# Gated cross-attention with two mixture-of-experts layers: moving the narrow products of TensorE directly behind the scores

## The chip, the core and the metric

The kernel runs on one core of a Trainium2 chip. The metric is the device time of one execution in microseconds (us). Its engines are TensorE (PE; its weight loads are listed as PEld), VectorE (DVE), ScalarE (ACT), GpSimd (POOL) and SyncE (SP, which issues transfers). Each runs its own list of instructions in order, and they wait for each other by semaphores.

## What is computed

Input x has 64 batches of 64 rows of 128 features. Two layers follow each other; each is a cross-attention to a context of the same shape, with 16 heads of 8 features, and then a mixture of experts. Layer one masks keys and sends each row to one of 8 experts (128 to 512 to 128); layer two has no mask and sends each row to two of 16 experts (128 to 64 to 128), with a capacity per expert and batch.

```
x = x + tanh(g_xattn[0]) * attention_0(layernorm(x), ctx, mask)
x = x + tanh(g_ffn[0])   * top1_experts(layernorm(x))
x = x + tanh(g_xattn[1]) * attention_1(layernorm(x), ctx)
x = x + tanh(g_ffn[1])   * top2_experts(layernorm(x))
```

Attention is softmax(Q K^T / sqrt(8)) V per head, with projections of x and ctx in front and an output projection behind.

## The kernel before

The 4,096 rows are 32 tiles of 128 rows (two batches each). A layer's attention loop goes over its 32 tiles; tiles 0 to 31 are layer one, 32 to 63 layer two. Tiles are gathered in groups of 2 or 4 (`SIZES`), and a group has units of two tiles. Products that are made for a whole group are the projections Q (L841) and K (L753), the transposes of x (L794), of the attention result (L896, "av") and of the router's input (L804), the output product (L903), the router's logits (L814) and the products that rank rows by expert (L823 to L835). V is projected per unit (L764). Per tile there are:

- the scores (L860): products of 32 rows by 64 columns of the array into the banks S_ps; layer one first writes the mask into the same banks with four full-array products (L854);
- four passes of VectorE over the scores: maximum and subtraction (L604, L612) for the first half of the heads, then for the second. `score` of the next tile waits for all of them, since S_ps is not doubled;
- the turn: four full-array transposes of the probabilities of one half of the heads (L871) into the one bank T_ps; ScalarE's exponential (L534) takes them from there to SBUF. Either half has a turn, and each waits until the exponential of the turn before has read the bank;
- A.V (L886): 32 products of 128 rows by 32 columns into A_ps, with the sum of the weights in two extra columns. VectorE divides (L620, L623).

All products read f32 operands except the mask's and the ranking's, which are bf16. A f32 product is recorded as two loads and two matmuls, a transpose or a bf16 product as one of each.

The order on an engine is not made by a scheduler. Each engine has a list of steps (step, items, time); `run` (L158) sorts all items by time and, at equal times, by the place of their step in the list. Times count in tiles: at time i stand the scores of tile i+1, the second half's turn of tile i, A.V of tile i-1, and the first half's turn of tile i+1. So in TensorE's list the places alone set the order within an iteration. `hook` adds the steps of the expert stages that run beside the loop's end.

```
            steps = [score_ahead] + awake + [(turn_probs(1), tiles, shift(0)),
                     (rank if masked else rank_slots, groups, settled(7 if masked else 8, 12, short, later)), (attend, tiles, shift(1)), (logit, groups[:7], settled(6, 9, short, later)),
                     (turn_av, groups, tail(2)), (project_q, groups, head(-2)), (output, groups, tail(3)),
                     (logit, groups[7:], settled(6, 9, short, later)),
                     (project_v, late_units, unit_head(-1)), (project_k, late, head(-3)),
                     (turn_probs(0), tiles, shift(-1)), (turn_r, groups, settled(5, 8, short, later)), (turn_x, groups, turn_x_at)]
```

With groups of four tiles, an iteration in four has V, ranking and the router's transposes; the next logits, V and the transposes of x; the next av and K; the next Q and the output product. In ScalarE's list the exponential of the second half stood first, then the copies of ranks and of logits (`keep_ranks`, `keep_logits`), of av, Q, V and K, and then the exponential of the first half. Early units of layer two have their V projected ahead of the loop by the same `project_v`.

Of the kernel before, what the change touches and what calls it, by code (L numbers as in the profile page):

```python
# [13 lines left out]
B, S, D = 64, 64, 128  # L14
# [3 lines left out]
P = 128  # L18
# [20 lines left out]
def wait(eng, sem, value):  # L39

    if not (isinstance(value, int) and value <= 0):
        eng.wait_ge(sem, value)
# [80 lines left out]
def head(skew):  # L123
    return lambda g: g.first + skew


def tail(skew):
    return lambda g: g.last + skew


def shift(skew):
    return lambda t: t + skew


def unit_head(skew):
    return lambda u: u.group.first + skew + u.k
# [13 lines left out]
def lag(g):  # L150
    return 1 if g.own > LAST_GROUPS else len(g.units)


def settled(skew, steady, short, later=()):
    return lambda g: g.last + (steady if g.own < short else lag(g) + skew + (g.own in later))
# [28 lines left out]
def attention(nc, ctx, space, x_all, r_xn, ws, dram, rs, hooks):  # L184

    R = 4
    CR = 3
# [3 lines left out]
    QUARTER = P // 4  # L191
# [17 lines left out]
    ctxT = sb("ctxT", [P, CR, Q, P])  # L209
# [42 lines left out]
    V_ps = Q_ps[:, :, :].rearrange("p u (b j d) -> p u b j d", b=2, j=HP)  # L252
# [65 lines left out]
    def of(layer):  # L318
        w, r, hook = ws[layer], rs[layer], hooks[layer]
        masked = layer == 0  # L320
        E = E0 if masked else E1
        short = 3 if masked else LAST_GROUPS
        later = (3, 4, 6) if masked else ()
        groups = GROUPS[layer * NG:(layer + 1) * NG]
        units = [u for g in groups for u in g.units]
        tiles = range(layer * NT, (layer + 1) * NT)
        early = [] if masked else groups[:3]
        late = [g for g in groups if g not in early]
        early_units = [u for g in early[:2] for u in g.units]
        late_units = [u for u in units if u not in early_units]  # L330
# [157 lines left out]
        def scalar_steps(act):  # L488
            def k_out(g):
                act.wait_ge(k_made, g.i + 1)  # L490
                wait(act, kblk_ready, tiles_to(g.i - R))
                nc.scalar.activation(kT[:, g.at(R), 0:g.n, :], Q_ps[:, 0:g.n, :], ACT.Identity, bias=w["bk"][:, 0:1]).then_inc(kT_ready, 1)  # L492

            def v_out(u):
                g, at = u.group, slice(2 * u.k, 2 * u.k + u.n)
                act.wait_ge(v_made, u.i + 1)
                act.wait_ge(zeroed, 3)
                wait(act, av_made, tiles_to(g.i - R))
                for s in range(2):
                    half = slice(s * S, (s + 1) * S)  # L500
                    last = nc.scalar.copy(v_blk[half, g.at(R), at, :, :, 2 + s * DK:2 + (s + 1) * DK].rearrange("p u b j d -> p (u b j) d"),  # L501
                                          V_ps[half, at, :, :, :].rearrange("p u b j d -> p (u b j) d"))
                last.then_inc(v_ready, 1)

            return k_out, v_out
# [5 lines left out]
        def scalar(act):  # L511
# [18 lines left out]
            def exp(h):  # L530
                def step(t):
                    act.wait_ge(probs_turned, 2 * t + h + 1)
                    wait(act, av_made, t - 1)
                    nc.scalar.activation(probT[:, t % 2, 4 * h:4 * h + 4, :], T_ps[:, :, :], ACT.Exp, scale=SCALE).then_inc(probT_ready, 1)  # L534
                return step
# [45 lines left out]
            def raise_(g):  # L581
                act.wait_ge(gap_ready, 2 * (g.own + 1))
                nc.scalar.activation(r["gap"][:, g.local:g.local + g.n], r["gap"][:, g.local:g.local + g.n], ACT.Exp).then_inc(raised_done, 1)
                for t in range(g.local, g.local + g.n):
                    if t > 1:
# [2 lines left out]
                                         accum_out=r["total"][:, t:t + 1]).then_inc(raised_done, 1)  # L588

            k_out, v_out = scalar_steps(act)  # L590
            steps = [(exp(1), tiles, shift(0)), (keep_ranks, groups, settled(7 if masked else 8, 12, short, later)), (keep_logits, groups, settled(6, 9, short, later)), (avT_out, groups, tail(2)), (q_out, groups, head(-2)),
                     (v_out, late_units, unit_head(-1)), (k_out, late, head(-3)),
                     (exp(0), tiles, shift(-1)), (r_xnT_out, groups, settled(5, 8, short, later)), (xnT_out, groups, turn_x_at), (normed, tiles, normed_at), (r_normed, units, lambda u: settled(4, 7, short, later)(u.group))]
            if not masked:
# [1 line left out]
            run(hook["first_scalar"](act) + steps + hook["scalar"](act))  # L596

        main.scalar, ahead.scalar = scalar, scalar_ahead

        def vector(dve):  # L600
# [147 lines left out]
        def tensor_steps(pe, bank):  # L748
            def project_k(g):
                pe.wait_ge(ctx_loaded[g.at(CR)], 16 * (g.i // CR + 1))  # L750
                pe.wait_ge(w["in_a"], 16)
                bank.take(kT_ready, g.i + 1)
                nc.tensor.matmul(Q_ps[:, 0:g.n, :], w["wk"][:, :], ctxT[:, g.at(CR), 0:g.n, :], start=True, stop=True).then_inc(k_made, 1)  # L753

            def project_v(u):
                g = u.group
                wv = w["wv"][:, :].rearrange("p (j r d) -> p j r d", j=HP, r=2)
                pe.wait_ge(ctx_loaded[g.at(CR)], 16 * (g.i // CR + 1))
                pe.wait_ge(w["in_b"], 16)
                bank.take(v_ready, u.i + 1)  # L760
                for k in range(2 * u.k, 2 * u.k + u.n):
                    for b in range(2):
                        for s in range(2):
                            last = nc.tensor.matmul(V_ps[s * S:(s + 1) * S, k, b, :, :], ctxT[:, g.at(CR), k, b * S:(b + 1) * S],  # L764
                                                    wv[:, :, s, :], start=True, stop=True, skip_group_check=True)
                last.then_inc(v_made, 1)

            return project_k, project_v

        def stream_into(bank, n):  # L770
            eye = w["ident"][:, :]
            nc.tensor.matmul(bank[:, 0:n, :], eye, eye.unsqueeze(1).to_broadcast([P, n, P]), start=True, stop=True)
# [10 lines left out]
        def tensor(pe):  # L783
# [4 lines left out]
            project_k, project_v = tensor_steps(pe, q_bank)  # L788
# [76 lines left out]
            def turn_probs(h):  # L865
                def step(t):
                    pe.wait_ge(shifted, 2 * t + h + 1)
                    wait(pe, probT_ready, 2 * t + h)
                    for j in range(4):
                        pair = prob[:, t % 2, 8 * h + 2 * j:8 * h + 2 * j + 2, :].rearrange("p r k -> p (r k)")  # L870
                        last = nc.tensor.transpose(T_ps[:, j, :], pair, ident[:, :])  # L871
                    last.then_inc(probs_turned, 1)
                return step
# [25 lines left out]
            def output(g):  # L899
                pe.wait_ge(r["bias_ready"], 1)  # L900
                x_bank.take(y_added, g.i + 1)
                for u in range(g.n):
# [3 lines left out]
            score_ahead = (score, tiles, score_at)  # L906
            awake = [] if masked else [(lambda n: stream_into(T_ps, n), [Q // 2], lambda _, when=when: when) for when in (NT - 3.95, NT - 1.99)]
            awake += [] if masked else [(lambda n: stream_into(T_ps, n), [Q], lambda _: NT - 1)]
            steps = [score_ahead] + awake + [(turn_probs(1), tiles, shift(0)),
                     (rank if masked else rank_slots, groups, settled(7 if masked else 8, 12, short, later)), (attend, tiles, shift(1)), (logit, groups[:7], settled(6, 9, short, later)),  # L910
                     (turn_av, groups, tail(2)), (project_q, groups, head(-2)), (output, groups, tail(3)),
                     (logit, groups[7:], settled(6, 9, short, later)),
                     (project_v, late_units, unit_head(-1)), (project_k, late, head(-3)),
                     (turn_probs(0), tiles, shift(-1)), (turn_r, groups, settled(5, 8, short, later)), (turn_x, groups, turn_x_at)]
            run(hook["first_tensor"](pe) + steps + hook["tensor"](pe))

        main.tensor, ahead.tensor = tensor, tensor_ahead
        return main, ahead

# [940 lines left out]
```

## Time and profile before

| | us |
|---|---|
| median of 3 runs | 525.49 |
| lowest and highest of the runs | 525.44, 529.74 |
| span of the profiled execution, first to last instruction | 522.8 |
| TensorE busy, matmuls | 446.0 |
| VectorE busy | 367.3 |
| ScalarE busy | 321.4 |
| GpSimd busy | 273.2 |

The profile is one execution. Only its span is known of it; what lies around the span is taken from the difference to the median of the runs, 2.7 us. A busy time counts the recorded instructions; "[idle before <-releaser]" behind a row of the timeline is the idle time of that engine before it and what ended it, and "issue" there means that the profile shows nothing it waited for. "xN" is the number of records merged in a row. The attention loop of layer one runs from about 16 to 180 us, the experts of layer one to about 280, the loop of layer two to about 435, and the second experts to the end.

### The profile page before, as it was taken

What the parts mean: (1) busy time and instruction counts of PE and PEld (TensorE: products, weight loads), DVE (VectorE), ACT (ScalarE), POOL (GpSimd) and SP (SyncE); (2) the same over time, 40 slices, a digit from 0 to 9 for tenths busy, and PEclk for the clock granted to TensorE, in tenths of its full rate; (3) what the DMA queues carried; (4) which work ended last, traced back from release to release, by engine and by line L of the source; (5) the groups of instructions that cost most, each with busy time, mean ns of one, the idle gap of its engine ahead of it and who ended that gap; (6) DMA issues with size and microseconds to landing.
All of it is one profiled execution on the core that took longest, in us unless ns stands there. A gap on an engine that the chain in (4) does not pass through costs nothing.

```text
span 522.8 us, 22052 instructions
## 1 busy us (share of the span) xinstructions
PE 446.0 (85%) x8481; PEld 325.6 (62%) x8481; DVE 367.3 (70%) x977; ACT 321.4 (61%) x764; POOL 273.2 (52%) x325
## 2 busy tenths in 40 slices
PE   2788899799978795999999689997897787889996
PEld 1455676566756585999984466665665565545554
DVE  5678788979787766355542779989898787544555
ACT  2355576566755773677754566767767467675653
POOL 2622534655474358888886435453444326534454
PEclk9999999999999988899999899999999999598999
DMA  7123444242111144665445010110031000000112
GB/s 204 50 55 114 109 124 122 61 113 69 45 39 37 40 98 104 89 94 73 48 37 153 2 43 5 43 34 23 3 84 35 21 4 3 2 1 6 41 51 68
DMA packets 50630, 30.69 MB, mean 59 GB/s; under 512 B 12384, under 2 KB 46944, under 8 KB 50528
## 3 DMA queue, kind: packets, MB, share of 16 engines
q1 hardware_dynamic: 37072, 18.54, 13.4%
q0 software_dynamic: 6640, 4.67, 7.0%
q10 hardware_dynamic: 6816, 6.07, 4.3%
q8 instruction: 70, 1.15, 0.9%
q14 instruction: 32, 0.26, 0.2%
HBM read 19.41 MB, written 9.85 MB: 56 GB/s over the span
## 4 chain that ended last, share of the span: by engine, by line
PE 45%; DVE 21%; issue 16%; POOL 7%; ACT 4%; DMA 3%; ACTq 1%; DVEq 1%; SPq 0%; POOLq 0%
DVE maxes L604 8%; PE T_ps L871 6%; PE S_ps L860 6%; POOL x_mid L1153 5%; PE A_ps L886 4%; PE m_H_ps L1464 3%; PE S_ps L854 2%; PE m_X_ps L1491 2%; PE m_T_ps L1504 2%; DVE prob L612 2%; PE f_H_ps L1205 2%; PE Q_ps L753 2%; PE Q_ps L841 2%; PE m_X_ps L1475 2%; PE m_X_ps L1447 2%
## 5 line engine op out<-in xcount | busy, mean ns | idle before, releaser
L604 DVE TENSOR_REDUCE maxes<-S_ps 128x8 f32<-128x512 f32 x128 | 87.5, 684 | 40.6 <-PE S_ps L860 40.6
L431 POOL TENSOR_TENSOR k_blk<-kT,col_a 128x512 f32<-128x512 f32 x64 | 67.9, 1070 | 82.1 <-ACT kT L492 57.9
L534 ACT ACTIVATE probT<-T_ps 128x512 f32<-128x512 f32 x128 | 76.1, 595 | 46.8 <-PE T_ps L871 46.0
L612 DVE TENSOR_TENSOR prob<-S_ps,maxes 128x512 f32<-128x512 f32 x128 | 88.5, 691 | 4.4
L871 PE MATMUL T_ps<-col_a,prob 128*128 128x128 f32 x512 | 83.1, 285 | 9.0 <-DVE prob L612 5.2
L871 PEld LDWEIGHTS T_ps<-col_a,prob 128*128 128x128 f32 x512 | 56.7, 143 | 46.9 <-issue 34.4
L1153 POOL DMA_INDIRECT x_mid<-f_out,f_rows x39 | 60.9, 1562 | 11.9 <-issue 10.7
L860 PE MATMUL S_ps<-k_blk,qT 32*64 32x256 f32 x1024 | 46.6, 411 | 5.3 <-DVE prob L612 4.5
L1018 DVE TENSOR_TENSOR f_hid<-f_H_ps,f_b 128x512 f32<-128x512 f32 x39 | 26.9, 691 | 33.3 <-PE f_Y_ps L1219 27.9
L886 PE MATMUL A_ps<-v_blk,probT 128*32 128x18 f32 x4096 | 48.4, 187 | 0.4 <-issue 0.4
L886 PEld LDWEIGHTS A_ps<-v_blk,probT 128*32 128x32 f32 x4096 | 41.8, 110 | 9.7 <-issue 8.9
L1205 PE MATMUL f_H_ps<-f_rowsT,f_w_now 128*128 128x128 f32 x312 | 43.2, 283 | 5.0 <-ACT f_rowsT L1164 5.0
L1219 PE MATMUL f_Y_ps<-f_w,f_hid 128*128 x312 | 42.5, 280 | 1.2 <-ACT f_hid L1176 1.0
L1205 PEld LDWEIGHTS f_H_ps<-f_rowsT,f_w_now 128*128 128x128 f32 x312 | 39.9, 200 | 5.2 <-ACT f_rowsT L1164 5.2
L1219 PEld LDWEIGHTS f_Y_ps<-f_w,f_hid 128*128 128x128 f32 x312 | 38.8, 195 | 1.9 <-issue 1.7
L468 POOL DMA_INDIRECT sorted_rows<-r_xn,row x32 | 32.1, 1005 | 15.0 <-DVE row L684 8.2
L501 ACT COPY v_blk<-Q_ps 64x256 f32<-64x256 f32 x64 | 23.9, 373 | 21.2 <-PE Q_ps L764 20.8
L517 ACT ACTIVATE xn<-x_all,shift_by,rstd 128x128 f32<-128x128 f32 x64 | 31.1, 493 | 9.4 <-DVE shift_by L642 9.4
L1384 POOL TENSOR_SCALAR m_other<-row_constants,r_slot,r_gap 128x128 f32<-128x128 f32 x32 | 25.4, 800 | 18.2 <-DVE m_combine L1353 17.6
L1176 ACT ACTIVATE f_hid<-f_hid 128x512 f32<-128x512 f32 x39 | 24.6, 631 | 16.4 <-DVE f_hid L1018 16.3
L453 POOL TENSOR_TENSOR x_all<-x_all,row_constants 128x512 f32<-128x512 f32 (+1 forms) x20 | 21.1, 1057 | 25.9 <-ACT xn L517 21.5
L460 POOL TENSOR_SCALAR r_spread<-r_stats 128x4 f32<-128x4 f32 (+1 forms) x20 | 3.9, 195 | 57.0 <-DVE r_stats L653 57.0
(202 smaller groups left out, 881.2 us busy)
## 6 DMA issues: line engine op xcount, KB each, us to landing
f_w<-in_W ACTq DMA_DIRECT2D x16, 256.0 KB, 2.8
ctxT<-in_ctxT SPq DMA_DIRECT2D x12, 256.0 KB, 3.1
f_rows<-sorted_rows SPq DMA_DIRECT2D x39, 64.5 KB, 2.0
out<-m_final SPq DMA_DIRECT2D x32, 64.0 KB, 1.5
x_all<-in_x SPq DMA_DIRECT2D x6, 256.0 KB, 5.7
x_mid<-x_all SPq DMA_DIRECT2D x6, 256.0 KB
x_all<-x_mid SPq DMA_DIRECT2D x6, 256.0 KB, 3.6
ctxT<-in_ctxT SPq DMA_DIRECT2D x8, 128.0 KB, 3.1
```

Of the source, the lines that this page charges most:

```text
L431: nc.gpsimd.tensor_tensor(k_blk[:, t % 2, :, :, :], kT[:, g.at(R), t - g.first, :].rearrange("p (b k) -> p b k", b=2).unsqueeze(2).to_broa ...
L468: pool.indirect_dma_start(r["sorted"], bass.IndirectOffsetOnAxis(ap=row[:, t:t + 1], axis=0), r_xn[:, t, :], None).then_inc(scattered[t >= ...
L517: nc.scalar.activation(xn[:, g.at(XR), u, :], x_of(t), ACT.Identity, bias=shift_by[:, g.i % NR, u:u + 1], scale=rstd[:, g.i % NR, u:u + 1] ...
L534: nc.scalar.activation(probT[:, t % 2, 4 * h:4 * h + 4, :], T_ps[:, :, :], ACT.Exp, scale=SCALE).then_inc(probT_ready, 1)
L604: nc.vector.tensor_reduce(maxes[:, t % 2, h, :, :], half_of(h), X, ALU.max).then_inc(max_ready, 1)
L612: nc.vector.tensor_tensor(prob[:, t % 2, heads, :].rearrange("p (r e) k -> p r e k", r=2), half_of(h), maxes[:, t % 2, h, :, :].unsqueeze( ...
L860: last = nc.tensor.matmul(S_ps[q // 2][b * S:(b + 1) * S, q % 2, 0:HQ * S], qT[rows, g.at(R), u, b * S:(b + 1) * S], k_blk[rows, t % 2, b, ...
L871: last = nc.tensor.transpose(T_ps[:, j, :], pair, ident[:, :])
L886: last = nc.tensor.matmul(AV[queries, m + j, :], probT[:, t % 2, j, queries], v_blk[:, g.at(R), t - g.first, c * part // S, j, :], start=T ...
L1153: pool.indirect_dma_start(r["x_mid"], bass.IndirectOffsetOnAxis(ap=rows[:, t % RINGS, D:RW].bitcast(I32), axis=0), out[:, t % DEEP, :], No ...
L1205: last = pe.matmul(H_ps[t % 2][:, n, :], w1_now[:, t % 2, n * P:(n + 1) * P], rowsT[:, t % 2, :], start=True, stop=True)
L1219: last = pe.matmul(Y_ps[t % 2][:, 0:D], hid[:, t % 2, n, :], w2[:, bass.ds(e, 1), n, :].rearrange("p a c -> p (a c)"), start=n == 0, stop= ...
```

## The change

TensorE's list: A.V, the logits of the first seven groups and V stand directly behind the scores; the turn of the second half, the ranking, av, Q, the output product, the late logits, K and the turn of the first half follow. V is made in products of 32 columns of the array (four column groups, `tile_position`) instead of 64. ScalarE's list: the copy of those logits goes ahead of the exponential. The file is one line longer from L764 on, so that later lines have numbers one higher.

```
-            steps = [(exp(1), tiles, shift(0)), (keep_ranks, groups, settled(7 if masked else 8, 12, short, later)), (keep_logits, groups, settled(6, 9, short, later)), (avT_out, groups, tail(2)), (q_out, groups, head(-2)),
+            steps = [(keep_logits, groups[:7], settled(6, 9, short, later)), (exp(1), tiles, shift(0)), (keep_ranks, groups, settled(7 if masked else 8, 12, short, later)), (keep_logits, groups[7:], settled(6, 9, short, later)), (avT_out, groups, tail(2)), (q_out, groups, head(-2)),
...
-                        for s in range(2):
-                            last = nc.tensor.matmul(V_ps[s * S:(s + 1) * S, k, b, :, :], ctxT[:, g.at(CR), k, b * S:(b + 1) * S],
-                                                    wv[:, :, s, :], start=True, stop=True, skip_group_check=True)
+                        for c in range(P // QUARTER):
+                            rows, keys = slice(c * QUARTER, (c + 1) * QUARTER), slice(b * S + c % 2 * QUARTER, b * S + (c % 2 + 1) * QUARTER)
+                            last = nc.tensor.matmul(V_ps[rows, k, b, :, :], ctxT[:, g.at(CR), k, keys], wv[:, :, c // 2, :], start=True,
+                                                    stop=True, skip_group_check=True, tile_position=(0, c * QUARTER))
...
-            steps = [score_ahead] + awake + [(turn_probs(1), tiles, shift(0)),
-                     (rank if masked else rank_slots, groups, settled(7 if masked else 8, 12, short, later)), (attend, tiles, shift(1)), (logit, groups[:7], settled(6, 9, short, later)),
+            steps = [score_ahead] + awake + [(attend, tiles, shift(1)), (logit, groups[:7], settled(6, 9, short, later)),
+                     (project_v, late_units, unit_head(-1)), (turn_probs(1), tiles, shift(0)),
+                     (rank if masked else rank_slots, groups, settled(7 if masked else 8, 12, short, later)),
                      (turn_av, groups, tail(2)), (project_q, groups, head(-2)), (output, groups, tail(3)),
-                     (logit, groups[7:], settled(6, 9, short, later)),
-                     (project_v, late_units, unit_head(-1)), (project_k, late, head(-3)),
+                     (logit, groups[7:], settled(6, 9, short, later)), (project_k, late, head(-3)),
                      (turn_probs(0), tiles, shift(-1)), (turn_r, groups, settled(5, 8, short, later)), (turn_x, groups, turn_x_at)]
```

TensorE, iterations 52 and 53, before. S_ps are scores, T_ps the turns, A_ps A.V, X_ps with "both" the ranking, Q_ps from ctxT the V projection, X_ps from r_xnT the logits, from r_xn and xn the transposes; the last number is how many products stand in a row:

```order
L860 MATMUL S_ps<-k_blk,qT 64x256 x8
L871 MATMUL T_ps<-col_a,prob 128x128 x4
L834 MATMUL X_ps<-both,before_bf 128x128
L835 MATMUL X_ps<-both,ones_bf 128x64
L886 MATMUL A_ps<-v_blk,probT 32x18 x32
L764 MATMUL Q_ps<-col_55,ctxT 64x64 x8
L871 MATMUL T_ps<-col_a,prob 128x128 x4
L804 MATMUL X_ps<-col_a,r_xn 128x128 x4
L860 MATMUL S_ps<-k_blk,qT 64x256 x8
L871 MATMUL T_ps<-col_a,prob 128x128 x4
L886 MATMUL A_ps<-v_blk,probT 32x18 x32
L814 MATMUL X_ps<-col_b,r_xnT 32x16 x16
```

In iteration 53 V, the turn of the first half and the transposes of x follow. The same place after the change, up to the transposes of iteration 53:

```order
L887 MATMUL A_ps<-v_blk,probT 32x18 x32
L765 MATMUL Q_ps<-col_55,ctxT 32x64 x16
L872 MATMUL T_ps<-col_a,prob 128x128 x4
L835 MATMUL X_ps<-both,before_bf 128x128
L836 MATMUL X_ps<-both,ones_bf 128x64
L872 MATMUL T_ps<-col_a,prob 128x128 x4
L805 MATMUL X_ps<-col_a,r_xn 128x128 x4
L861 MATMUL S_ps<-k_blk,qT 64x256 x8
L887 MATMUL A_ps<-v_blk,probT 32x18 x32
L815 MATMUL X_ps<-col_b,r_xnT 32x16 x16
L765 MATMUL Q_ps<-col_55,ctxT 32x64 x16
L872 MATMUL T_ps<-col_a,prob 128x128 x8
```

A.V, logits and V now stand behind the scores without a full-array product between them, V has 16 products a unit instead of 8, and in iteration 53 the two turns follow each other ("x8").

ScalarE, iterations 52 and 53, before (probT is the exponential, v_blk the copy of V, r_xnT that of the router's transposes, r_logits that of the logits):

```order
L501 COPY v_blk<-Q_ps 64x32x8 x2
L534 ACTIVATE probT<-T_ps 128x512
L553 COPY r_xnT<-X_ps 128x512
L517 ACTIVATE xn<-x_all,shift_by,rstd 128x128
L583 ACTIVATE r_gap<-r_gap 128x4
L587 ACTIVATE raised,r_total<-r_logits,low 128x16 x4
L534 ACTIVATE probT<-T_ps 128x512
L562 COPY r_logits<-X_ps 128x64
L501 COPY v_blk<-Q_ps 64x32x8 x2
```

The same place after the change:

```order
L501 COPY v_blk<-Q_ps 64x32x8 x2
L534 ACTIVATE probT<-T_ps 128x512
L553 COPY r_xnT<-X_ps 128x512
L517 ACTIVATE xn<-x_all,shift_by,rstd 128x128
L583 ACTIVATE r_gap<-r_gap 128x4
L587 ACTIVATE raised,r_total<-r_logits,low 128x16 x4
L562 COPY r_logits<-X_ps 128x64
L534 ACTIVATE probT<-T_ps 128x512
L501 COPY v_blk<-Q_ps 64x32x8 x2
```

The copy of the logits stands ahead of the exponential of the second half now; the copy of V still stands behind it.

## Rows read from the trace of the kernel before

**Rows 1.** The page: span, busy time by engine, the chain by engine.
```profile
span 522.8 us, 22052 instructions
...
PE 446.0 (85%) x8481; PEld 325.6 (62%) x8481; DVE 367.3 (70%) x977; ACT 321.4 (61%) x764; POOL 273.2 (52%) x325
...
PE 45%; DVE 21%; issue 16%; POOL 7%; ACT 4%; DMA 3%; ACTq 1%; DVEq 1%; SPq 0%; POOLq 0%
```

**Rows 2.** Timeline, iteration 53: start, us, engine, line, operation, tiles, [idle before <-releaser].
```profile
377.56 0.69 PE L860 MATMUL S_ps<-k_blk,qT 32*64 32x256 f32 x16 [0.32 <-DVE prob L612]
...
378.18 0.66 PE L871 MATMUL T_ps<-col_a,prob 128*128 128x128 f32 x4
...
378.34 0.69 DVE L604 TENSOR_REDUCE maxes<-S_ps 128x8 f32<-128x512 f32 x1 [0.59 <-PE S_ps L860]
...
378.77 0.74 PE L886 MATMUL A_ps<-v_blk,probT 128*32 128x18 f32 x64
...
379.37 0.45 PE L814 MATMUL X_ps<-col_b,r_xnT 128*32 128x16 f32 x32
...
379.74 0.70 PE L764 MATMUL Q_ps<-col,ctxT 128*64 128x64 f32 x16
...
380.38 0.66 PE L871 MATMUL T_ps<-col_a,prob 128*128 128x128 f32 x4
380.39 0.69 DVE L612 TENSOR_TENSOR prob<-S_ps,maxes 128x512 f32<-128x512 f32 x1
...
380.87 0.60 PE L794 MATMUL X_ps<-col_a,xn 128*128 128x128 f32 x4
...
381.40 1.29 PE L860 MATMUL S_ps<-k_blk,qT 32*64 32x256 f32 x16
...
383.75 0.69 DVE L604 TENSOR_REDUCE maxes<-S_ps 128x8 f32<-128x512 f32 x1
```

**Rows 3.** Timeline, iteration 41, where the subtraction releases the next scores.
```profile
323.64 0.69 PE L860 MATMUL S_ps<-k_blk,qT 32*64 32x256 f32 x16 [0.31 <-DVE prob L612]
...
326.48 0.69 DVE L612 TENSOR_TENSOR prob<-S_ps,maxes 128x512 f32<-128x512 f32 x1
...
327.32 0.69 PE L860 MATMUL S_ps<-k_blk,qT 32*64 32x256 f32 x16
...
328.15 0.67 DVE L604 TENSOR_REDUCE maxes<-S_ps 128x8 f32<-128x512 f32 x1
```

**Rows 4.** Timeline, iteration 44: turn, exponential, turn.
```profile
335.33 0.60 PE L871 MATMUL T_ps<-col_a,prob 128*128 128x128 f32 x4
...
335.97 0.60 ACT L534 ACTIVATE probT<-T_ps 128x512 f32<-128x512 f32 x1 [0.64 <-PE T_ps L871]
...
336.71 0.63 PE L871 MATMUL T_ps<-col_a,prob 128*128 128x128 f32 x4 [0.16 <-ACT probT L534]
```

**Rows 5.** The page's DMA queues: packets, MB, share of 16 engines.
```profile
q8 instruction: 70, 1.15, 0.9%
```

**Rows 6.** Timeline of TensorE at four stops, and at K in iteration 28.
```profile
104.14 0.23 PE L814 MATMUL X_ps<-col_b,r_xnT 128*32 128x8 f32 x3 [1.70 <-issue]
...
361.71 0.37 PE L814 MATMUL X_ps<-col_b,r_xnT 128*32 128x16 f32 x20 [1.18 <-issue]
...
366.01 0.24 PE L886 MATMUL A_ps<-v_blk,probT 128*32 128x18 f32 x3 [0.44 <-issue]
...
414.91 0.70 PE L764 MATMUL Q_ps<-col,ctxT 128*64 128x64 f32 x15 [0.68 <-issue]
...
161.17 0.67 PE L753 MATMUL Q_ps<-ctxT,col_a 128*128 128x256 f32 x2 [0.95 <-ACT v_blk L501]
```

**Rows 7.** DMA queues in the window 101.7 to 102.9, then 102.9 to 104.2.
```profile
q8 instruction: 1, 0.02, 5.3%
...
q0 software_dynamic: 1, 0.00, 0.0%
```

## Prediction

> **What bounds the kernel now.** I read the page's sums and its chain first, then the timeline of single iterations of the attention loop (an iteration is named by the tile t, 0 to 63, whose scores open it; 32 to 63 are layer two), then TensorE's stalls and the queue that brings its instructions. TensorE is busy 85% of the span and VectorE 70%, and the chain that ended last is split between them, with 16% under "issue" [rows 1]. So neither engine is the bound everywhere; what counts is which one ends an iteration.
>
> Iteration 53 shows it [rows 2]. Its scores start at 377.56; maxima and subtractions run on VectorE from 378.34 to 381.08 (380.39 + 0.69); TensorE meanwhile turns probabilities (378.18), does A.V (378.77), logits (379.37), V (379.74), the next turn (380.38) and the x transposes (380.87); the next scores start at 381.40. The loop scores, four VectorE passes, scores is 0.78 + 2.74 + about 0.15 = 3.67 us in layer two (4.27 in layer one, where four mask products stand ahead of the scores), and TensorE's list is about as long. Iteration 41 is such a case with VectorE the bound: last subtraction 326.48 + 0.69 = 327.17, scores at 327.32, 3.68 after its own [rows 3]. By the starts of scores and ends of subtractions in the timeline, 38 of the 62 steps from one tile to the next end like this, within 0.35 us of the subtraction. In those, TensorE time that is saved is worth nothing, and TensorE time that is added counts as soon as the list passes 3.67.
>
> **Part one: the A.V, logits and V move ahead of the turn of the second half.** A full-array block that follows another starts 0.49 after it (turn to x: 380.87 - 380.38), A.V in 32 columns starts 0.59 after the same turn (378.77 - 378.18) [rows 2]. So a change between products of different array shape costs about 0.10 us. In program order, four steady iterations have 18 such changes before and 12 after. That shortens TensorE's list by 0.1 in an iteration without V, by 0.2 with it. It is worth something only where TensorE ended the iteration and VectorE is free when the scores come: seven iterations (10, 11, 23, 35, 39, 42, 50), 0.1 each and 0.3 in 39, where the turn waited for ScalarE as well and now comes later anyway: **-0.9 us**. In the others that TensorE ends (43, 47, 51, 55) VectorE is still at router work when the scores are done.
>
> What it gives away: both turns of an iteration write the one bank T_ps, and ScalarE's exponential must read the first before the second may start. Turn, exponential, turn is 335.33, 335.97 + 0.60, 336.71: 1.38 us from start to start against 0.49 without the wait [rows 4]. Before, A.V and V (1.2 us) stand between the two and hide it. After, where no av, q, output or K product stands between, nothing does, and VectorE's cover (its first subtraction, some 2.2 after the scores) ends too early. Iteration 41 then reads: scores 0, A.V 0.62, V 1.22, turn 1.86, second turn 3.24, x 3.73, next scores 4.26 instead of 3.68; the maxima of tile 42 start 0.83 after its scores, 0.05 later than they could, so 0.55 is lost. Steady V iterations all carry the router's or x's transposes behind the second turn. Six of them have no other slack and no instruction stall (9, 12, 36, 40, 41, 44: 0.5, 0.2, 0.15, 0.15, 0.55, 0.5): **+2.05 us**. In 8, 13, 45 and 56 the next tile's VectorE work or the mask's 0.6 hides it: nothing.
>
> **Part two: V in products of 32 columns.** The moving side stays 64 wide, and four column groups work side by side instead of two, so a V block still takes about 0.6; I cost its array time at nothing (bounds: the 0.60 of the 64-column block as it is, [rows 2], and twice that if the four groups did not overlap, which A.V's 64 records in 0.6 speak against). But its instructions double. Each tile's V is 8 products now, not 4, each of them two loads and two matmuls: 64 tiles x 4 x 4 = 1,024 more instructions on TensorE.
>
> That matters because TensorE's instructions arrive by DMA: 70 packets, 1.15 MB [rows 5], 16 KB each, for 2 x 8,481 records [rows 1] and 988 waits and register instructions, 17,950 in all, so 256 in a packet. TensorE stops four times in the attention loop with only "issue" to show for it: 1.70 in the logits at 104.14, 1.18 in logits at 361.71, 0.44 in A.V at 366.01, 0.68 in V at 414.91 [rows 6]; the stretched scores of 54 (1.29 at 381.40, [rows 2]) are a fifth. A packet starts and lands inside 101.7 to 102.9, and none moves until the resumption at 104.14 [rows 7]; in all five cases TensorE resumes 1.2 to 1.35 after the landing, 2.3 after the packet's start. Counting instructions in program order, the packet starts 0.2 to 1.0 us after each 256th instruction, and all five stops fall 192 instructions behind a multiple of 256. So the rule of this trace: 192 instructions that run in less than about 2.95 us (0.6 + 2.35) stop TensorE until 2.95 is over. In the loop no stretch of the old order below 2.8 escaped it.
>
> The new order makes a dense burst: scores 32, A.V 128, logits 64, V 64 instructions with nothing between them, 288 within 2.2 us. I laid the multiples of 256 on the new order (18,974 instructions, four packets more). In 12 iterations the 192 that follow one lie wholly inside the burst: 2, 16, 17, 20, 21, 24, 25, 28, 30, 52, 53 and 57. Worked for 53: packet asked for at 0.2, TensorE stops in the logits until 3.15; V 3.2, turn 3.85, second turn 5.23, x 5.72, next scores 6.25 instead of 3.84, so 2.4 late. The maxima of 54 started 2.35 after its scores where 0.78 would do [rows 2], because VectorE had router work; 1.57 is absorbed, 0.8 lost. The same sum gives from 0.3 (30) to 2.0 (28, where K in addition waits for the copy of V, which before ended its 0.95 wait at 161.17 [rows 6], and which ScalarE now does behind the exponential of a later turn). All 12: 1.65 + 0.6 + 0.35 + 0.75 + 1.6 + 1.4 + 1.05 + 2.0 + 0.3 + 0.9 + 0.8 + 0.4 = **+11.8 us**. The old stops disappear or move; 17 is in the list with its difference alone, the one in 49 was absorbed by half and what follows it is bound by VectorE.
>
> The Trainium skill (Runtime: NRT & Kernel Launch, Instruction fetch mechanics) says the sequencer fetches the next 16 KiB block while it runs the current one, and calls the cost mostly hidden. By that sentence the 11.8 would be zero; the 16 KB agree with the packets here, the hiding does not in the five stops.
>
> ScalarE's order changes only in that the copy of early logits goes ahead of the exponential; the logits are made earlier too, so I cost it at nothing (if the logits stop for instructions, the exponential waits, but its turn stands behind them anyway). VectorE, GpSimd and SyncE keep their orders. Experts and the final stage have no changed block.
>
> **Sum.** 522.8 - 0.9 + 2.05 + 11.8 = 535.75 in the span. The median of the runs, 525.5, lies 2.7 above this span; with that, **538 us**, 2.4% slower.
>
> **Rivals.** (1) No added stops: packets are asked for early enough, as in most of the old iterations. Then the 12 iterations lose only the exponential's exposure (0.9 together) and iteration 17 wins back about 1: 525.5 - 0.9 + 2.05 + 0.9 - 1.0 = 526.5. For it: most lines of the old order get by. Against: none of the old order's tightest four did.
> (2) Faster: the array-shape changes decide. If TensorE were the bound of nearly every iteration, 16 x 6 x 0.10 = 9.6 us go: 516. It decides once the exponential is hidden and TensorE, not the subtraction, releases the scores; [rows 3] show the opposite, and TensorE's 85% in [rows 1] is all that speaks for it. The Trainium skill (TensorEngine Tiling (Array Packing), Key Properties) says that a change of tiling mode drains the engine; the 0.10 here agrees, and that rule alone would give this rival's time.
> (3) The stops cost more: also the stretches of 2.9 to 3.3 stop briefly, and V in four groups takes 0.2 longer in 30 iterations, half of them on the path: 538 + 5 + 3 = 546.
>
> **Chances.** Forecast 0.55, (1) 0.20, (2) 0.08, (3) 0.17. One per cent (5.3 us) is about what a measurement of this kernel can tell from no change. Faster by more than that: 0.08. Within it: rival (1), less its slow end, 0.18. Slower: 0.74. The range of 527 to 546 reaches from rival (1) to rival (3).
>
> **What would show it.** Right: 74 instruction packets; some ten "issue" gaps above 1 us on TensorE inside logits or V; in V iterations a second turn that waits for ScalarE's exponential, 1.4 behind the first; scores that start later than 0.35 after the last subtraction in most V iterations; A.V 0.62 after the scores; waits of the maxima for scores clearly above those of before. Wrong: no more than five such gaps, a V block much longer or shorter than 0.6, or scores still released by the subtraction in V iterations.

## The result and the profile after

The changed kernel takes 544.36 us (median of 4 runs, 540.85 to 545.83), the kernel before 526.35 beside it; the ratio is 1.0317, 95% interval 1.0272 to 1.0362. It is slower, as forecast (538, range 527 to 546), by more than the forecast: 18.0 us and not 12.5. Some executions on this chip are in a slower state, and the medians here leave them out.

The page of the changed kernel: span, TensorE's busy time, the chain by engine, and the queue that brings instructions.

```profile
span 543.7 us, 23076 instructions
...
PE 443.9 (82%) x8993; PEld 327.7 (60%) x8993; DVE 367.1 (68%) x977; ACT 318.6 (59%) x764; POOL 273.4 (50%) x325
...
PE 48%; DVE 17%; issue 15%; POOL 8%; ACT 6%; DMA 3%; ACTq 1%; DVEq 1%; SPq 1%; POOLq 0%
...
q8 instruction: 74, 1.21, 1.0%
```

Against [rows 1] TensorE's matmuls are busy for 2 us less, with 512 recorded matmuls more (256 products of V), and the span is 21 us longer: on balance the time is idle time. The four packets more are there [rows 5].

Where it lies is read from the starts of iterations 0, 31, 32 and 63 in the timelines (an iteration starts with its scores, in layer one with the mask's products ahead of them). Layer one's loop takes 174.3 us instead of 155.4 (+18.9), layer two's 143.4 instead of 141.4 (+2.0); the experts between and the end differ by 0.1. So nearly everything is lost in layer one. VectorE sees the same 21 us: its maxima wait for the scores for 61.6 us in all, before for 40.6 (us in total, times, longest; the changed kernel first):

```profile
DVE maxes L604 <- PE S_ps L861: 61.6, 47, 4.7
DVE maxes L604 <- PE S_ps L860: 40.6, 42, 3.2
```

Iteration 21, in layer one, holds the largest single loss, 8.54 us against 4.27. Its timeline from the scores on, TensorE alone (start, us, line, tiles, [idle before]):

```profile
127.00 0.69 PE L861 MATMUL S_ps<-k_blk,qT 32*64 32x256 f32 x16
127.61 1.07 PE L887 MATMUL A_ps<-v_blk,probT 128*32 128x18 f32 x64
128.54 0.37 PE L815 MATMUL X_ps<-col_b,r_xnT 128*32 128x8 f32 x22
130.31 0.29 PE L815 MATMUL X_ps<-col_b,r_xnT 128*32 128x8 f32 x10 [1.40 <-issue]
130.46 0.99 PE L765 MATMUL Q_ps<-col_b,ctxT 128*32 128x64 f32 x32
131.38 1.11 PE L872 MATMUL T_ps<-col_a,prob 128*128 128x128 f32 x4
133.28 1.09 PE L872 MATMUL T_ps<-col_a,prob 128*128 128x128 f32 x4 [0.78 <-ACT probT L534]
134.16 1.06 PE L795 MATMUL X_ps<-col_a,xn 128*128 128x128 f32 x4
135.01 1.06 PE L855 MATMUL S_ps<-mask_bias,ident_bf 128*128 128x256 bf16 x4
```

Three things happen one after the other. TensorE stops inside the logits with "issue" alone to show for it; the second turn then waits for the exponential of the first; and everything from V on takes nearly twice as long. The queues in the window 127.2 to 128.8 show the packet of the stop:

```profile
q8 instruction: 1, 0.02, 5.4%
```

No other follows before TensorE resumes at 130.31. The slow blocks are explained by the windows (us, busy times by engine, PEclk, DMA share, GB/s):

```profile
128.00:130.00 2.00, 0.85 (x62) 0.66 (x54) 1.93 (x4) 0.00 (x0) 1.97 (x2) 1.00 0.48 159
130.00:132.00 2.00, 1.69 (x45) 1.52 (x46) 1.93 (x6) 0.19 (x1) 1.27 (x3) 0.65 0.04 8
132.00:134.00 2.00, 1.22 (x7) 0.85 (x6) 0.86 (x6) 1.23 (x3) 1.74 (x2) 0.50 0.29 81
134.00:136.00 2.00, 2.00 (x10) 1.41 (x8) 0.00 (x0) 1.34 (x3) 0.41 (x1) 0.50 0.62 181
136.00:138.00 2.00, 2.00 (x82) 1.22 (x82) 0.70 (x2) 0.23 (x1) 0.00 (x0) 0.64 0.00 0
```

TensorE was busy 0.85 of the 2 us from 128 to 130, and from 130.6 the granted clock is at its lower level, 1.2 GHz (0.50), until 137.4. The prediction had nothing of this. The Trainium skill (TensorE: Matmul & The Clock Gate, Part 1: The HAM clock gate) says that an idle TensorE is taken back to half its clock; the trace agrees, with the 0.50 behind the stop. Not every stop is followed by it: behind the stop of 1.70 at 104.14 in the kernel before [rows 6] the granted clock stayed at 1.00. In layer one's loop the kernel before has full clock, the changed one does not:

```profile
16.00:172.00 156.00, 136.65 (x3324) 96.11 (x3325) 125.04 (x278) 92.85 (x202) 77.30 (x88) 1.00 0.29 79
```

```profile
16.00:172.00 156.00, 125.52 (x3192) 89.06 (x3193) 111.08 (x246) 82.21 (x181) 69.16 (x79) 0.97 0.27 75
172.00:191.00 19.00, 14.47 (x390) 10.14 (x391) 12.22 (x33) 8.38 (x19) 8.34 (x10) 0.91 0.12 35
```

The first row is the kernel before, the two others the changed one.

Iteration 53, which the prediction worked out, had no stop (TensorE, the exponential between the turns, and VectorE's last subtraction):

```profile
397.77 0.69 PE L861 MATMUL S_ps<-k_blk,qT 32*64 32x256 f32 x16 [0.32 <-DVE prob L612]
398.39 0.74 PE L887 MATMUL A_ps<-v_blk,probT 128*32 128x18 f32 x64
...
398.99 0.45 PE L815 MATMUL X_ps<-col_b,r_xnT 128*32 128x16 f32 x32
399.26 0.69 PE L765 MATMUL Q_ps<-col,ctxT 128*32 128x64 f32 x32
...
399.88 0.66 PE L872 MATMUL T_ps<-col_a,prob 128*128 128x128 f32 x4
...
400.57 0.60 ACT L534 ACTIVATE probT<-T_ps 128x512 f32<-128x512 f32 x1 [0.71 <-PE T_ps L872]
400.61 0.69 DVE L612 TENSOR_TENSOR prob<-S_ps,maxes 128x512 f32<-128x512 f32 x1
...
401.32 0.63 PE L872 MATMUL T_ps<-col_a,prob 128*128 128x128 f32 x4 [0.78 <-DVE prob L612]
...
402.31 0.69 PE L861 MATMUL S_ps<-k_blk,qT 32*64 32x256 f32 x16
```

V's block in 32 columns takes 0.62 from its start to the turn's (399.26 to 399.88), in 64 columns 0.64 [rows 2]: the products side by side cost no array time. The second turn starts 1.44 behind the first. Its row names the subtraction, but this turn needs the first half's alone, which ended at 399.97, and the exponential of the turn before it, which ended at 401.17 (400.57 + 0.60): so the exponential held it. The next scores start 4.54 behind these, 1.01 after the last subtraction (400.61 + 0.69) instead of 0.32.

TensorE's waits of the changed kernel and of the one before (us in total, times, longest):

```profile
PE T_ps L872 <- ACT probT L534: 12.7, 19, 0.8
...
PE X_ps L815 <- issue: 7.1, 5, 1.8
...
PE Q_ps L753 <- ACT v_blk L501: 5.5, 4, 1.7
...
PE Q_ps L765 <- issue: 4.7, 5, 1.5
```

```profile
PE Q_ps L753 <- ACT v_blk L501: 3.8, 4, 0.9
PE T_ps L871 <- ACT probT L534: 3.5, 14, 0.7
```

### The profile page after: what moved, and what is told of

The parts are those of the page before. It is cut to its first block, busy times and chain, and to the rows that moved or that the text cites. A ratio compares the mean times of both kernels' runs of the same rounds, so it can differ in the third digit from the quotient of the medians.

```text
span 543.7 us, 23076 instructions
## 1 busy us (share of the span) xinstructions
PE 443.9 (82%) x8993; PEld 327.7 (60%) x8993; DVE 367.1 (68%) x977; ACT 318.6 (59%) x764; POOL 273.4 (50%) x325
## 3 DMA queue, kind: packets, MB, share of 16 engines
q8 instruction: 74, 1.21, 1.0%
## 4 chain that ended last, share of the span: by engine, by line
PE 48%; DVE 17%; issue 15%; POOL 8%; ACT 6%; DMA 3%; ACTq 1%; DVEq 1%; SPq 1%; POOLq 0%
PE T_ps L872 8%; PE S_ps L861 7%; POOL x_mid L1154 6%; DVE maxes L604 6%; PE A_ps L887 5%; PE S_ps L855 3%; PE m_H_ps L1465 3%; PE Q_ps L765 2%; DVE prob L612 2%; PE m_X_ps L1492 2%; PE m_T_ps L1505 2%; PE f_H_ps L1206 2%; ACT probT L534 2%; PE Q_ps L753 2%; PE m_X_ps L1476 2%
## 5 line engine op out<-in xcount | busy, mean ns | idle before, releaser
L604 DVE TENSOR_REDUCE maxes<-S_ps 128x8 f32<-128x512 f32 x128 | 87.7, 685 | 61.8 <-PE S_ps L861 61.6
L872 PE MATMUL T_ps<-col_a,prob 128*128 128x128 f32 x512 | 84.9, 290 | 23.6 <-ACT probT L534 12.7
L1154 POOL DMA_INDIRECT x_mid<-f_out,f_rows x39 | 60.9, 1562 | 12.7 <-issue 9.7
L887 PEld LDWEIGHTS A_ps<-v_blk,probT 128*32 128x32 f32 x4096 | 43.0, 112 | 26.7 <-issue 25.5
L887 PE MATMUL A_ps<-v_blk,probT 128*32 128x18 f32 x4096 | 49.9, 188 | 1.2 <-issue 1.0
L861 PEld LDWEIGHTS S_ps<-k_blk,qT 32*64 32x64 f32 x1024 | 16.3, 135 | 19.8 <-issue 18.4
```

The source lines that it names most:

```text
L604: nc.vector.tensor_reduce(maxes[:, t % 2, h, :, :], half_of(h), X, ALU.max).then_inc(max_ready, 1)
L861: last = nc.tensor.matmul(S_ps[q // 2][b * S:(b + 1) * S, q % 2, 0:HQ * S], qT[rows, g.at(R), u, b * S:(b + 1) * S], k_blk[rows, t % 2, b, ...
L887: last = nc.tensor.matmul(AV[queries, m + j, :], probT[:, t % 2, j, queries], v_blk[:, g.at(R), t - g.first, c * part // S, j, :], start=T ...
L1154: pool.indirect_dma_start(r["x_mid"], bass.IndirectOffsetOnAxis(ap=rows[:, t % RINGS, D:RW].bitcast(I32), axis=0), out[:, t % DEEP, :], No ...
```

## The experiments

Theory A: the new order costs by stops for instructions, which depend on where the packets of 256 instructions fall, and by waits that lost their cover. Theory B: the order itself, or the number of V's products, costs the time wherever the packets fall. "Stops" below are TensorE's gaps over 0.3 us under "issue" ahead of A.V, logits, V or a turn, between 17 and 470 us of each run's timeline. The kernel before has four, 4.0 us in all; the changed one eleven, 12.7 us (the 14 of the first expectation is a count by a wider rule). In the thirteen traces there are 58 stops. Counted in TensorE's instructions in order of start, every one of them lies 193 to 195 behind a multiple of 256, whatever product stands there and whatever the padding, and ends 1.2 to 1.8 us after a packet's landing, 2.2 to 3.1 after its start.

**Padding, the order unchanged.** Tiny products ahead of the first real one, into a place that the real one overwrites; 24 of them are 96 instructions (18: 72, 32: 128, 48: 192, and so on):

```
             for n, w in enumerate((w0, w1)):
                 nc.tensor.wait_ge(bv_laid, n + 1)
+                for c in range(24 * (n == 0)):
+                    at = slice(c % 4 * 32, (c % 4 + 1) * 32)
+                    nc.tensor.matmul(Y_ps[at, 0:8], bv_rows[:, 0, at], w0["wo"][:, 0:8], start=True, stop=True, skip_group_check=True,
+                                     tile_position=(0, c % 4 * 32))
```

> The changed kernel with 24 tiny products (96 instructions, 8 columns, result overwritten) in front of the first real product of TensorE, where it idles anyway. Order and work of the loop are the same; only the place of the 256-instruction packets moves by 96. Theory A (stops for instructions): the multiples of 256 leave the burst of scores, A.V, logits and V in most iterations; laid on the trace of the changed kernel only 3 of its 14 stops remain, so 527 to 531 us. Theory B (the new order itself, the exposed exponential and the shape of the products, costs the 18 us): 544 to 546, as without the padding.

> The same with 48 tiny products, 192 instructions. Theory A: some nine full stops in other iterations than without padding, longer ones, 546 to 554 us. Theory B: 544 to 546 again, with whatever stops.

Measured: 537.17 us with 96 (ratio to before 1.0172, 1.0076 to 1.0269) and 555.40 with 192 (1.0553, 1.0479 to 1.0628), against 544.36 with none. The same work in the same order spans 18 us by alignment alone, which theory B can't give. Stops: 4 (5.5 us, none in layer one's loop) and 10 (14.9 us). Layer one's loop takes 160.1 us with 96 and 176.7 with 192, against 174.3 with none. Iteration 21 with 96, without a stop:

```profile
120.98 0.69 PE L861 MATMUL S_ps<-k_blk,qT 32*64 32x256 f32 x16
...
122.52 0.44 PE L815 MATMUL X_ps<-col_b,r_xnT 128*32 128x8 f32 x32
122.80 0.65 PE L765 MATMUL Q_ps<-col_b,ctxT 128*32 128x64 f32 x32
123.39 0.66 PE L872 MATMUL T_ps<-col_a,prob 128*128 128x128 f32 x4
124.82 0.63 PE L872 MATMUL T_ps<-col_a,prob 128*128 128x128 f32 x4 [0.78 <-ACT probT L534]
...
125.72 0.60 PE L855 MATMUL S_ps<-mask_bias,ident_bf 128*128 128x256 bf16 x4
```

From scores to the mask's products of the next tile it is 4.74 here and 8.01 in the fence above; 1.40 of the 3.27 is the stop, and nearly all of the rest lies in blocks at the lower clock (turn 0.66 against 1.11, V's 0.59 from start to turn against 0.92). The exposed 0.78 is the same in both. With 192, in iteration 13, the stop has moved from the logits into V, and the low clock follows it:

```profile
89.49 0.42 PE L765 MATMUL Q_ps<-col_b,ctxT 128*32 128x64 f32 x15
91.64 0.55 PE L765 MATMUL Q_ps<-col_b,ctxT 128*32 128x64 f32 x17 [1.73 <-issue]
92.12 1.11 PE L872 MATMUL T_ps<-col_a,prob 128*128 128x128 f32 x4
```

The kernel with 96 came out 6 above its range of 527 to 531: it has one stop more than counted (all four behind 349 us), low clock in layer one without a stop (a router transpose waited 2.08 for its input at 156.6, and the granted clock is 0.50 from 156.8 to 163.6), and the waits without cover, which theory A had too low. The kernel with 192 came out 1.4 above its range of 546 to 554.

**One half of the change at a time.** V in 64 columns in the new order; V in 32 columns in the old order (V's loop of the one file put into the other).

> The new order on TensorE and ScalarE, but V in products of 64 columns as before: 1,024 instructions less, four tiles of layer one are 945 to 963 instructions again instead of 1,009 to 1,027. Theory A: the packets rotate against the iterations, two full stops, and the exposed exponential of some 2 to 3 us stays: 526 to 530 us. Theory B (order): 540 to 545, since only V's products differ.

> The old order with V in products of 32 columns, so that the instructions and the packets are those of the changed kernel. Theory A: the turns between A.V, logits and V spread the instructions, so that about eight windows are short by 0.1 to 0.5 and one by 1.6 us: 526 to 530 us. If four column groups cost array time of their own, V blocks are longer than 0.6 and the time is above 530. Theory B in the form that V's split costs it: 540 and more.

Measured: 537.34 (1.0228, 1.0143 to 1.0313), stops 2; and 527.53 (1.0011, 0.9967 to 1.0054), stops 6. Splitting V alone costs nothing that can be measured in the time of ten runs, although it brings all the packets and 7.3 us of stops (in the one profiled run layer one's loop is 6.7 us longer, and the stages outside the loops are 2.5 shorter). Its multiples of 256 lie at the same places of the same iterations as in the changed kernel, so the order decides which of them stop. The order alone costs 11 us, above theory A's range and below theory B's. The two stops lie at 106.1 and 425.7 and are 2.9 us together, which doesn't make 11.

**The order without stops.** The same kernel with 6 tiny products:

> The new order with V in 64 columns (the run after_v64) and 6 tiny products, 24 instructions, in front. Laid on the trace of after_v64 no multiple of 256 is followed by 192 instructions in under 3.15 us then, so the two stops of that run (in the iterations at 102 and 421 us) should be gone, and with them the low clock behind the first. Theory A (stops, and the clock behind them): what is left is the exposed exponential less the saved changes of shape, some 1 to 3 us, and before has its own five stops: 526 to 530 us. Theory B (the order itself costs the 11 us of after_v64): 536 to 538.

Measured: 533.33 (1.0159, 1.0118 to 1.0200). Both theories missed. The two stops are gone, as counted; three short ones (1.7 us) are left; 8.4 us over the 524.96 beside it remain, not 1 to 3. The waits of this run and, in the second fence, of the next:

```profile
PE T_ps L871 <- ACT probT L534: 9.3, 14, 0.9
...
PE X_ps L896 <- ACT rank_now L568: 2.3, 3, 0.8
...
PE X_ps L896 <- ACT rank_now L572: 1.7, 2, 0.8
```

The second kind was not in the prediction: av's transposes follow the ranking directly now and wait for its copy out of the bank, where A.V stood between before (that wait does not occur in the kernel before; the changed kernel has the same 4.0 us of it). And in iteration 60 low clock follows waits alone, without any full stop; the granted clock is 0.50 from 417.8 for 13.7 us:

```profile
416.25 0.63 PE L804 MATMUL X_ps<-col_a,r_xn 128*128 128x128 f32 x4 [1.28 <-DVE x_all L631]
417.64 0.56 PE L794 MATMUL X_ps<-col_a,xn 128*128 128x128 f32 x2 [0.77 <-ACT r_xnT L553]
418.14 1.16 PE L860 MATMUL S_ps<-k_blk,qT 32*64 32x256 f32 x16
...
425.11 1.19 PE L753 MATMUL Q_ps<-ctxT,col 128*128 128x256 f32 x2 [1.42 <-ACT v_blk L501]
...
427.08 1.16 PE L860 MATMUL S_ps<-k_blk,qT 32*64 32x256 f32 x16
```

Scores to scores it is 8.94 there, 6.22 in the kernel before. K waits 1.42 for V's copy, which stands behind an exponential that comes later now.

**The cover put back.** The same kernel with V alone moved behind the turn and the ranking again, and the changed kernel itself with that edit:

```
-                     (project_v, late_units, unit_head(-1)), (turn_probs(1), tiles, shift(0)),
-                     (rank if masked else rank_slots, groups, settled(7 if masked else 8, 12, short, later)),
+                     (turn_probs(1), tiles, shift(0)), (rank if masked else rank_slots, groups, settled(7 if masked else 8, 12, short, later)),
+                     (project_v, late_units, unit_head(-1)),
```

> The run after_v64_pad24 (new order, V in 64 columns, no stop for instructions in the loop) with one edit: V goes back behind the turn of the second half and the ranking, so that it stands between the two turns again and, in ranking iterations, between the ranking and the turn of av. Theory A (the 8 us that this order loses without stops are waits that lost their cover: the second turn for the exponential, av for the copy of the ranks): some 4 to 6 us come back, 527 to 530 us, and the waits of the turn for the exponential in the loop of layer one fall from 5.3 to under 2.5 us. Theory B (A.V ahead of the turn is what costs): 532 to 534, as after_v64_pad24.

> The changed kernel (V in 32 columns, same packets) with V alone moved back behind the turn and the ranking. Theory A: the burst behind the scores is 64 instructions shorter and ends in a full-array turn, so that only the iterations with logits can still stop; the stops go from 14 to about six, the exposed waits to half: 530 to 536 us. Theory B (V's products of 32 columns cost by their number): 540 to 545.

Measured: 527.75 (1.0014, 0.9980 to 1.0049) and 532.61 (1.0111, 1.0044 to 1.0179), both as theory A had it. In the first, 5.6 us come back (533.33 - 527.75), and what remains over the kernel before is 1.5 of 8.4:

```profile
PE T_ps L871 <- ACT probT L534: 3.1, 10, 0.9
...
PE X_ps L896 <- ACT rank_now L568: 2.3, 3, 0.8
...
PE X_ps L896 <- ACT rank_now L572: 0.7, 1, 0.7
```

The second turn's wait is back at the level of before (3.1 us, before 3.5; in layer one 2.0, from 5.3), though two stops of 2.8 us in all came up that had not been counted. A.V ahead of the turn is therefore not what costs the 8 us. The gain is not in the waits alone: in the profiled runs 3.2 us of it lie in iterations 60 and 61, where the long stretch of low clock is gone. And av's waits for the ranks' copy are still 3.0 of 4.0 us, so this run does not show that they cost time. In the second, five stops are left of eleven, all but one of them above 1 us, all in iterations with logits, as expected.

**A.V alone, where V is not.** Can the changes of array shape be saved without losing the cover?

```
+            narrow = [t for t in tiles if t + 1 in {unit_head(-1)(u) for u in late_units}]
-            steps = [score_ahead] + awake + [(turn_probs(1), tiles, shift(0)),
-                     (rank if masked else rank_slots, groups, settled(7 if masked else 8, 12, short, later)), (attend, tiles, shift(1)), (logit, groups[:7], settled(6, 9, short, later)),
+            steps = [score_ahead] + awake + [(attend, [t for t in tiles if t not in narrow], shift(1)), (turn_probs(1), tiles, shift(0)),
+                     (rank if masked else rank_slots, groups, settled(7 if masked else 8, 12, short, later)), (attend, narrow, shift(1)), (logit, groups[:7], settled(6, 9, short, later)),
```

> The old order with one edit: in iterations without V, A.V stands directly behind the scores, ahead of the turn of the second half; with V nothing is changed, so V still hides the exponential. No instruction is added. Theory A: the saved changes of shape, 0.1 to 0.3 us in some ten iterations that TensorE ends, 1 to 2.5 us, less one or two new short stops: 523 to 527 us. If A.V ahead of the turn costs something of its own (a later second exponential), slower than before, 528 to 531.

> The kernel mixed with 4 tiny products, 16 instructions, in front: by the packets five short windows with 1.4 us in all, against eight with 3.3 us without the padding. Theory A: 1 to 4 us faster than mixed, 521 to 525. Theory B: as mixed.

Measured: 526.84 (1.0044, 1.0006 to 1.0081) and 526.30 (1.0028, 0.9992 to 1.0064), with 524.96 for the kernel before beside both. The expected gain did not come. By the timelines of the second, iterations 19 and 23 are 0.2 shorter each (4.50 for 4.69, 4.50 for 4.72), but iteration 20 is 0.45 longer. Larger losses are in 17 and 28, 1.43 and 1.20, where the granted clock fell to 0.50 (for 3.4 us from 104.5 and from 159.2); the kernel before had 1.00 in both. Why it fell here, behind a stop of 1.79 in 17 where the kernel before has one of 1.70, stays open.

**Padding of the kernel before.** 32 and 18 tiny products:

> The kernel before with 32 tiny products, 128 instructions, in front: by the packets two short windows (at 138 and 393 us) instead of four. Theory A: 0 to 3 us faster than before, 523 to 526. Theory B: as before, 526.

> The kernel before with 18 tiny products, 72 instructions, in front: by the packets five short windows with 4.0 us in all, at 119, 139, 338, 374 and 423 us, against 2.6 without and 1.7 with 128. Theory A: 1 to 5 us above before, 526 to 530, with stops at just those places. Theory B: as before, 525.

Measured: 522.41 (0.9944, 0.9909 to 0.9978), stops 2 (1.8 us), and 525.40 (0.9967, 0.9930 to 1.0003), stops 3 (3.2 us). The first beats the kernel before by 0.2 to 0.9%; one of its two stops was where it was counted (141.8), the other not (110.2). The second is a miss: of five windows only three stopped, and the time did not rise as theory A had it. With before_v32 (six stops, 7.3 us, no measurable cost) this speaks for later waits taking up most of a stop in the old order. How much the old order owes to its four stops is thus not settled by these two alignments.

## Why the prediction was right, and where it was wrong

- **Stops for instructions (+11.8): right in cause; in size part of the agreement is luck.** The cause is shown by the place of all 58 stops and by moving the packets, which moves the stops. The changed kernel lies 11.0 us above its order without full stops (544.36 - 533.33; 9.6 when each is set against the kernel before beside it). But by stage the number is two errors that cancel. In layer one's loop the changed kernel takes 174.3, its order with 96 instructions in front, where none stops, 160.1, and after_v64_pad24, with one stop of 0.44, 159.7; so some 14 us go to stops and the low clock behind them, where the prediction has 9.7 for iterations 2 to 30 (by the order of its list). In layer two's loop the changed kernel is 4.8 shorter than after_v64_pad24 (143.4 and 148.3), whose iteration 60 fell into low clock. Of the twelve iterations eight stopped: 2, 17, 20, 21, 24, 25, 28, 57. Four did not (16, 30, 52, 53), and 12, 13 and 26 stopped unforeseen.
- **The step that failed there** is "the packet starts 0.2 to 1.0 us after each 256th instruction". In all four iterations that did not stop, the packet starts 1.9 to 3.1 us ahead of its multiple. That of iteration 53 starts at 394.76, 3.0 us ahead of the scores in which the multiple lies, and behind it the second turn of iteration 52 waits 1.21; the queue's row of the window 394 to 396.3 is

```profile
q8 instruction: 1, 0.02, 3.9%
```

  In 13 and 26, which stopped unforeseen, the packet starts 3.0 and 2.6 us behind its multiple; 12 stopped for 0.33 with a stretch of 2.85, inside the prediction's own 2.95. The trace of before had early packets too, one at 401.68, ahead of the scores at 404.65 in which its multiple lies. So in iteration 53 a new wait may have saved a new stop; in 16, 30 and 52 long full-array products (Q, the output product) run behind the packet's start instead. What sets how early or late a packet starts was not tried. Also, "2.3 after the packet's start" is 2.3 to 2.6 for the stops of before.
- **Each stop costs more than worked out.** The idle itself is 12.7 us in eleven stops; the prediction had no low clock behind a stop, and iterations 21, 25 and 28 lost 4.27, 3.07 and 3.27 where it had 1.6, 1.05 and 2.0 (the first two by the order of its list).
- **Waits without cover (+2.05): the term that was mis-sized.** The order without full stops costs 8.4 us. Of this 3.7 lie in iterations 60 and 61 in the profiled run, which the low clock reached and the prediction did not name. The six iterations of the term (9, 12, 36, 40, 41, 44) are 3.1 us longer there instead of 2.05, and "In 8, 13, 45 and 56 the next tile's VectorE work or the mask's 0.6 hides it: nothing" failed: these are 0.30, 0.73, 0.82 and 0.67 longer. The waits of av for the ranks' copy (4.0 us) were not seen at all; what they cost was not separated.
- **Saved changes of shape (-0.9): there in its iterations, but no net gain shown.** In after_v64_pad24 the seven iterations of the term are together 0.97 shorter than before. Iterations 43, 47, 51 and 55, where the prediction expected nothing, are 1.57 shorter, but the next ones (44, 48, 52, 56; the first and the last are among those with the waits above) 2.27 longer. The two runs with A.V ahead alone bring no net gain.
- **V in 32 columns: right** (nothing in array time). In the new order with hardly a stop, layer one's loop takes the same with either V, 160.1 and 159.7 us.
- **Layer one** was hit because of a coincidence that the prediction did not name: counted in the programs, four steady tiles of layer one are 1,009 to 1,027 instructions after the change (945 to 963 before), four packets almost exactly, so that the multiples of 256 fall into the same place of the burst again and again (16, 20, 24, 28 and 17, 21, 25). In layer two they are 970 to 974 and drift, and only one full stop came.
- **Rivals.** (1) and (2) are excluded by the interval. (3) named the time (546) better than the forecast, but not by its mechanism: V's blocks are no longer than before, and the three stretches of 2.9 to 3.3 us behind a multiple in the changed kernel have no stop.
- **Its own signs.** Most came: 74 packets; 22 of 30 iterations with V are followed by a start later than 0.35 after the last subtraction (11 before); the second turn 1.44 behind the first; A.V 0.62 after the scores; longer waits of the maxima. One came only just: six gaps above 1 us in logits or V (a seventh has 1.00), where some ten were to show it right and no more than five wrong.

The Trainium skill (Runtime: NRT & Kernel Launch, Instruction fetch mechanics) calls the fetch mostly hidden. The runs here agree only where the 193 instructions behind a multiple of 256 last until the packet is in, 2.2 to 3.1 us after its start in the 58 stops; where they often did not, the same loop took 537 to 555 us by its alignment.

## What to carry to other kernels

Products that are free in array time still cost instructions: count the instructions of one period of the loop, and keep dense runs of short products under a packet's worth or break them with long ones. If a change of order costs more than its waits explain, shift it by some tiny products first: the alignment alone can be worth more than the order. And before gathering work of one kind, ask what it was standing between: here V hid an exponential, and A.V a copy whose price was not separated.

## What the runs showed of the hardware

- A packet of instructions late by 1.4 us cost 3.3 us in iteration 21, since the granted clock fell to 0.50 for 6.8 us behind it; without a full stop, it fell behind waits of 1.28 and 0.77 us in iteration 60. It did not fall behind a stop of 1.70 in the kernel before.
- Ninety-six instructions that do nothing, ahead of everything, took 7 us off; 192 added 11.
- TensorE's stops for instructions, as counted here, have one fixed place, 193 to 195 instructions behind a multiple of 256, in all 58 cases. In the changed kernel's loops a packet started anywhere from 3.1 us ahead of its multiple, where no stop came, to 3.2 us behind it.
